# Selective scan: both rows copied to SBUF by ScalarE, and half of the B product on GpSimd in 18 of 64 units

## The reference, cut to what matters

```
states = states * exp(dt_t[:, :, None] * A) + dt_t[:, :, None] * B_t[:, None, :] * x_t[:, :, None]
y = einsum('bdn,bn->bd', states, C_t)
```

## Time and profile before

| | us |
|---|---|
| median of three runs | 2974.84 |
| lowest and highest run | 2967.43, 2976.77 |
| span of the profiled execution | 2973.1 |
| VectorE busy in the span | 2498.2 |
| state loop: first to last `times_b` starts | 2116.6 to 2364.2 |
| `times_b` L1864, 64 of them, busy | 76.8 |
| scans L1875, 128 of them, busy | 157.3 |
| `times_c` L1681, 63 of them, busy | 148.0 |

### The profile page before, as it was taken

One profiled execution on the slowest core, in us unless ns is written; L12 is line 12 of the kernel. 1 busy time (PEld: TensorE's weight loads), 2 busy tenths in 40 slices (PEclk: granted clock), 3 DMA queues, 4 the chain that ended last, 5 costly groups with the idle time before them and its releaser, 6 DMA issues.

```text
span 2973.1 us, 58047 instructions
## 1 busy us (share of the span) xinstructions
PE 2792.8 (94%) x23085; PEld 1251.6 (42%) x23085; DVE 2498.2 (84%) x3270; ACT 2081.2 (70%) x3906; POOL 881.3 (30%) x1050
## 2 busy tenths in 40 slices
PE   8999999999999989999999999999888799978889
PEld 2222222235666632222222356666333265467755
DVE  8999999976777689999999767776799956899854
ACT  6999999975666569999999766665777423735232
POOL 1000000012343310000000123433388655199810
PEclk9999999999999999999999999999999999989999
DMA  2000000000000010000000000000000000000000
GB/s 94 7 16 18 17 18 16 14 8 1 2 1 2 2 54 6 17 16 17 17 17 15 12 1 1 1 2 2 27 1 0 10 1 1 0 1 1 1 1 15
DMA packets 29148, 33.62 MB, mean 11 GB/s; under 512 B 13195, under 2 KB 23438, under 8 KB 28622
## 3 DMA queue, kind: packets, MB, share of 16 engines
q1 hardware_dynamic: 28878, 29.92, 3.5%
HBM read 17.58 MB, written 7.34 MB: 8 GB/s over the span
## 4 chain that ended last, share of the span: by engine, by line
PE 68%; DVE 19%; ACT 6%; issue 3%; POOL 2%; DMA 0%; SPq 0%; DVEq 0%; POOLq 0%; PEldq 0%; ACTq 0%
PE banks L401 15%; PE banks L383 10%; DVE max_parts L528 7%; PE banks L376 5%; PE banks L1114 3%; PE banks L2147 2%; PE banks L1025 2%; PE banks L2132 2%; PE banks L2134 2%; PE banks L1088 2%; PE banks L1133 2%; PE banks L1057 2%; ACT probs L644 2%; DVE banks L2998 2%; DVE state_keys L2995 2%
## 5 line engine op out<-in xcount | busy, mean ns | idle before, releaser
L528 DVE TENSOR_REDUCE max_parts<-banks 128x2 f32<-128x1024 f32 x1024 | 1170.7, 1217 | 11.5 <-PE banks L376 9.9
L644 ACT ACTIVATE probs<-banks 128x512 f32<-128x512 f32 x2048 | 1085.3, 599 | 59.8 <-PE banks L383 33.2
L383 PE MATMUL banks<-q_parts,k_parts 51*128 51x512 bf16 x2048 | 654.6, 385 | 4.8 <-ACT v_heads L603 1.5
L401 PE MATMUL banks<-probs,v_heads 128*9 128x256 f32 x8192 | 637.7, 383 | 8.2 <-ACT pv_copy L655 2.0
L376 PE MATMUL banks<-k_parts,q_parts 48*128 48x512 bf16 x2048 | 595.5, 385 | 10.5 <-DVE max_parts L528 6.0
L383 PEld LDWEIGHTS banks<-q_parts,k_parts 51*128 51x128 bf16 x2048 | 151.8, 94 | 474.7 <-ACT probs L644 397.1
L711 POOL CAST neg_max_parts<-neg_max 128x8 bf16<-128x8 f32 x64 | 13.0, 203 | 1122.5 <-DVE neg_max L533 1122.5
L401 PEld LDWEIGHTS banks<-probs,v_heads 128*9 128x9 f32 x8192 | 123.4, 88 | 382.0 <-issue 343.0
L1681 POOL TENSOR_TENSOR state_times_c<-state,c_row 128x1024 f32<-128x1024 f32 x63 | 148.0, 2354 | 88.8 <-ACT c_row L1997 54.2
L1875 DVE TENSOR_TENSOR_SCAN state<-banks,state_carry,state 128x512 f32<-128x512 f32 x128 | 157.3, 1271 | 6.4 <-ACT banks L1992 4.3
L2318 ACT ACTIVATE silu_a<-banks 128x512 f32<-128x512 f32 x80 | 47.7, 597 | 163.0 <-PE banks L2132 162.8
(11 more groups left out here) (526 smaller groups left out, 5053.3 us busy)
## 6 DMA issues: line engine op xcount, KB each, us to landing
outT_half<-pv_copy SPq DMA_DIRECT2D x248, 16.0 KB
prob_sums<-pv_copy SPq DMA_DIRECT2D x248, 2.0 KB
q_scratch<-qk_parts SPq DMA_DIRECT2D x8, 384.0 KB, 2.5
k_scratch<-qk_parts SPq DMA_DIRECT2D x8, 384.0 KB, 2.6
k_parts<-k_scratch SPq DMA_DIRECT2D x28, 96.0 KB
q_parts<-q_scratch SPq DMA_DIRECT2D x28, 96.0 KB
q_parts<-neg_max_rows SPq DMA_DIRECT2D x128, 3.0 KB
ffn_weights<-moe SPq DMA_DIRECT2D x1, 1928.0 KB, 7.6
```

Source lines behind the costliest of these rows:

```text
L383: nc.tensor.matmul(bank("exp", n, x)[:, :], K[p % 2][half_of(x, ROWS + PARTS), tile(t)], Q[p % 2][half_of(x, ROWS + PARTS), blk(j)], start ...
L401: i = nc.tensor.matmul(PVb[group:group + VD, cols], V[:, t + k, 2 * (s // NB) + x, :], PT[:, (n + k) % RING, x, cols], start=(t == 0 and c ...
L528: nc.vector.tensor_reduce(mxp[s % 2][:, :, u // NB, u % NB], Mb[m % 2].rearrange("p (x k) -> p x k", x=2), AX.X, ALU.max).then_inc(*maxed. ...
L644: nc.scalar.activation(PT[:, n % RING, x, :], bank("exp", n, x)[:, :], ACT.Exp, scale=float(HD) ** -0.5).then_inc(*exped.inc())
```

## The change

- The B row and the C row of a unit are spread by TensorE into two neighbouring banks (`spread`), two units ahead instead of one.
- ScalarE copies both rows with one 128x1024 copy to SBUF (`copy_bc`), in place of the 128x512 copy of the C row alone, also two units ahead, into one of four buffers `rows_of`.
- `times_b`, `times_c` and the last product read the rows from there. So `times_b` has both inputs in SBUF, and TensorE no longer waits for `times_b`, only for the copy.
- In 18 units GpSimd makes the upper half (c = 1) of the B product (`times_b_upper`), and VectorE's `times_b` only the lower. These are the units 2, 8 and 14 of the first block, 0, 2, 8 and 14 of the next two, and 0, 2, 6, 8, 10, 12 and 14 of the last. On GpSimd it is placed ahead of the `times_c` of the unit before. The second scan of a unit waits for it.

The diff, cut to its core:

```diff
+SHARED_WITH_FRONT, SHARED_IN_LAST = (0, 2, 8, 14), (0, 2, 6, 8, 10, 12, 14)
...
-        Cs, y = two("c_row", [128, 512]), two("scan_out", [128, 2, 512])
+        rows_of, y = [sb(f"bc_rows{i}", [128, 2, 512]) for i in range(4)], two("scan_out", [128, 2, 512])
...
-        Eb, Bb, Cb, Yb = g.ps[0:3], g.ps[3], g.ps[4], g.ps[5:7]
+        Eb, BCb, Yb = g.ps[0:3], g.wide(3), g.ps[5:7]
...
+        shared = [m for m in range(1, M) if m % NS in (SHARED_WITH_FRONT if m // NS + 1 < NB else SHARED_IN_LAST)]
+        n_shared = lambda m: len([k for k in shared if k <= m])
...
+            def times_b_upper(m):
+                pool.wait_ge(bc_copied, m + 1)
+                pool.wait_ge(dtx_made, m // NS + 1)
+                pool.wait_ge(c_times_state, m - 2)
+                pool.wait_ge(carried, m - 2)
+                nc.gpsimd.tensor_tensor(F[m % 3][:, 1, :], dtx[:, 1, unit_blk(m)], rows_of[m % 4][:, 0, :], ALU.mult).then_inc(*b_times_upper_x.inc())
...
             for m in range(M - 1):
                 b, n = m // NS, m % NS
+                if m + 1 in shared:
+                    times_b_upper(m + 1)
                 times_c(m)
...
-            def spread_b(m):
+            def spread(m):
                 pe.wait_ge(bc_low, m // NS + 1)
                 pe.wait_ge(mid_made, m // NS + 1)
-                pe.wait_ge(b_times_x, m)
-                nc.tensor.matmul(Bb[:, :], sel[:, m % NS, :], BC[:, unit_blk(m)], start=True, stop=True).then_inc(*b_spread.inc())
-
-            def spread_c(m):
-                pe.wait_ge(c_copied, m)
-                nc.tensor.matmul(Cb[:, :], sel[:, NS + m % NS, :], BC[:, unit_blk(m)], start=True, stop=True).then_inc(*c_spread.inc())
+                pe.wait_ge(bc_copied, m)
+                for k in range(2):
+                    i = nc.tensor.matmul(BCb[:, blk(k)], sel[:, NS * k + m % NS, :], BC[:, unit_blk(m)], start=True, stop=True)
+                i.then_inc(*bc_spread.inc())
...
             def times_b(m):
-                dve.wait_ge(b_spread, m + 1)
+                dve.wait_ge(bc_copied, m + 1)
                 dve.wait_ge(dtx_made, m // NS + 1)
                 dve.wait_ge(c_times_state, m - 2)
                 dve.wait_ge(carried, m - 2)
-                nc.vector.tensor_tensor(F[m % 3][:, :, :], dtx[:, :, unit_blk(m)], Bb[:, :].unsqueeze(1).broadcast_to([128, 2, 512]),
+                k = 1 if m in shared else 2
+                nc.vector.tensor_tensor(F[m % 3][:, 0:k, :], dtx[:, 0:k, unit_blk(m)], rows_of[m % 4][:, 0, :].unsqueeze(1).broadcast_to([128, k, 512]),
                                         ALU.mult).then_inc(*b_times_x.inc())
...
                     dve.wait_ge(decay_made, 2 * m + c + 1)
+                    if c == 1:
+                        dve.wait_ge(b_times_upper_x, n_shared(m))
...
-            def copy_c(m):
-                act.wait_ge(c_spread, m + 1)
-                act.wait_ge(c_times_state, m - 1)
-                nc.scalar.copy(Cs[m % 2][:, :], Cb[:, :]).then_inc(*c_copied.inc())
+            def copy_bc(m):
+                act.wait_ge(bc_spread, m + 1)
+                act.wait_ge(c_times_state, m - 3)
+                nc.scalar.copy(rows_of[m % 4][:, :, :].rearrange("p k t -> p (k t)"), BCb[:, :]).then_inc(*bc_copied.inc())
...
             decay(0)
-            copy_c(0)
+            copy_bc(0)
+            copy_bc(1)
```

More of the change, by code:

```diff
@@ L1624, in mamba @@
          dt_projected, dt_read, e_made, one_plus, log_made, u_back, rests_made, logs_made, dt_made, dtx_made) = s_front
-        s_loop = g.signals("b_spread c_spread decay_made c_copied b_times_x scanned carried c_times_state summed y_made y_gated last_product last_gated out_made x_added")
-        b_spread, c_spread, decay_made, c_copied, b_times_x, scanned, carried, c_times_state, summed, y_made, y_gated, last_product, last_gated, out_made, x_added = s_loop
+        s_loop = g.signals("bc_spread decay_made bc_copied b_times_x b_times_upper_x scanned carried c_times_state summed y_made y_gated last_product last_gated out_made x_added")
+        bc_spread, decay_made, bc_copied, b_times_x, b_times_upper_x, scanned, carried, c_times_state, summed, y_made, y_gated, last_product, last_gated, out_made, x_added = s_loop
         readers = dict(v0=(read_out, 4, 1), v1=(read_out, 4, 2), p2=(read_out, 4, 3), p3=(read_out, 4, 4),
@@ L1675, in times_x @@
                 nc.gpsimd.tensor_tensor(dtx[:, :, blk(b)], dt[:, :, blk(b)], xi[:, :, blk(b)], ALU.mult).then_inc(*dtx_made.inc())
+            def times_b_upper(m):
[4 more added lines that the diff above has]
+                nc.gpsimd.tensor_tensor(F[m % 3][:, 1, :], dtx[:, 1, unit_blk(m)], rows_of[m % 4][:, 0, :], ALU.mult).then_inc(*b_times_upper_x.inc())
             def times_c(m):
                 pool.wait_ge(scanned, 2 * m + 2)
-                pool.wait_ge(c_copied, m + 1)
+                pool.wait_ge(bc_copied, m + 1)
                 pool.wait_ge(summed, 2 * (m - 1))
-                nc.gpsimd.tensor_tensor(G[m % 2][:, :, :], F[m % 3][:, :, :], Cs[m % 2][:, :].unsqueeze(1).broadcast_to([128, 2, 512]),
+                nc.gpsimd.tensor_tensor(G[m % 2][:, :, :], F[m % 3][:, :, :], rows_of[m % 4][:, 1, :].unsqueeze(1).broadcast_to([128, 2, 512]),
                                         ALU.mult).then_inc(*c_times_state.inc())
@@ L1798, in on_pe @@
             pe.wait_ge(selected, 1)
-            spread_b(0)
-            spread_c(0)
+            spread(0)
+            spread(1)
             for m in range(M):
                 b, n = m // NS, m % NS
-                if m + 1 < M:
-                    spread_b(m + 1)
-                    spread_c(m + 1)
+                if m + 2 < M:
+                    spread(m + 2)
                 if b + 1 < NB:
@@ L1889, in last_product_of @@
                 dve.wait_ge(scanned, 2 * m + c + 1)
-                dve.wait_ge(c_copied, m + 1)
+                dve.wait_ge(bc_copied, m + 1)
                 dve.wait_ge(summed, 2 * (m - 1))
-                nc.vector.tensor_tensor(G[m % 2][:, c, :], F[m % 3][:, c, :], Cs[m % 2][:, :], ALU.mult).then_inc(*last_product.inc())
+                nc.vector.tensor_tensor(G[m % 2][:, c, :], F[m % 3][:, c, :], rows_of[m % 4][:, 1, :], ALU.mult).then_inc(*last_product.inc())
             def gate_last(c):
@@ L2033, in on_act @@
                     decay(m + 1)
-                    copy_c(m + 1)
+                    if m + 2 < M:
+                        copy_bc(m + 2)
                 if b + 1 < NB:
```

## The result

Four executions of the changed kernel took 3016.11 to 3025.56 us, median 3019.6, against 2974.32 for four of the kernel before on the same chip: a ratio of 1.0162, 95% interval 1.0145 to 1.0179, or 45.3 us more. The kernel is slower, as forecast, inside the range, and 14 us beyond the number predicted. The profiled execution took 3018.72 us, its span 3017.4, which is 44.3 over the span of the earlier trace rows. All of it lies in the state loop: the loop is 47.2 us longer, and what stands ahead of it was 3.3 shorter in this execution. First the page of the kernel after: the span, and busy time by engine.

The account below looks back on a forecast made before the run. VectorE, with next to no room in the state loop, was taken as the bound. Losses from blocking, less the waits that go, summed to +30.8 us on 2974.84: 3005.6 us, 8-in-10 range 2968 to 3024.

Parts of the forecast that it names:

- The question that decides: State loop: whether a VectorE product with two SBUF inputs and a GpSimd product exclude each other; claimed they do.
- A plain unit: State-loop unit without other GpSimd work behind `times_c`: costs nothing, `times_c` done at 3.38, before the next `times_b` at 3.60.
- The 15 long operations: `rests`, `correct_log`, `add_log`, `times_x` and `gate` on GpSimd behind `times_c`: 1.95 us lost each, 29.2 in all.
- The two splits: `split_rest` and `split_low` on GpSimd, 1.26 us each: cost 0.85 us each, six times, 5.1 in all.
- the waiting VectorE instruction goes first: Between two GpSimd instructions, a held VectorE product gets in, though the next GpSimd one started 0.04 us before.
- `add_x`: In two blocks of the state loop, hides about 0.6 us of the loss behind `split_rest` and `split_low`: -1.2 us.
- The halves: The 18 shared units: 15 lose 0.27 us each, 4.1 in all; three beside `finish` gain 0.53 each, -1.6.
- The decay of unit 3: VectorE's wait there grows about 0.5 us in two blocks, 0.2 in the last, shrinks 0.3 in the first: +0.9.
- What goes: VectorE's waits in the state loop that disappear: 6.0 us for the B row and 2.0 for the sums.
- The one without exclusion: Rival: no exclusion for this pair in the state loop, so 13.2 us faster, 2962 us; chance 0.12.
- the other rival: Rival: no exclusion, but the engines beside VectorE cap the state loop's gain at -7, 2968 us; chance 0.06.
- GpSimd gets there first: Rival: `times_c` wins at each scan's end, a unit takes 5.99 us, about 3125 us in all; chance 0.03.

Follow-up runs that it names:

- the rows alone: The changed kernel without the 18 shared halves, all 64 units reading both rows from SBUF: 3022.13 us, ratio 1.0159 to the kernel before.
- All three runs: Against the changed kernel: splits on 128 partitions, 3014.7 us; a completion wait behind each split, 3011.06 us; `rests` on 32 partitions in three blocks, 3041.02 us.
- the kernel with the added waits: The changed kernel with GpSimd waiting for the completion of each `split_rest` and `split_low` before going on: 3011.06 us, ratio 1.0125.
- The kernel with the short copies: The changed kernel with ScalarE copying the C row alone for units 2 and 3 of the three later blocks: 3022.54 us in one run.
- the kernel that writes zeros ahead of it: The changed kernel with `split_rest` and `split_low` on 128 partitions instead of 32, the added ones holding zeros: 3014.7 us, ratio 1.0134.

## Why the prediction was right, and where its sum was not

**The question that decides** was settled as predicted. With the rows in SBUF the pair excludes each other, with the B row in PSUM it does not, and the rows alone cost as much as the whole change. That the time lies inside the range is in part luck: the range's upper end stood for no overlap at all; the overlap was there, and the time came near that end by other terms.

**A plain unit** costs nothing: 3.61 us, `times_c` at 3.25 where 3.38 - 0.16 = 3.22 was worked out.

**The 15 long operations** at 1.95 us: `rests` and `correct_log` lengthen their unit by 1.98 to 2.00, six times. Of the 0.15 of overlap most held as well: `times_b` ends 1.08 behind `rests`, 0.12 less than its 1.20. Beside the Trainium skill (SBUF — State Buffer, section "Who interferes with whom"), whose rule taken literally came to 43 us, the measured 45 us are a near hit for another reason: the exclusion is as it says, the missing overlap is not, and what lifts the time to that number is the next term.

**The two splits are the step that failed.** The prediction had "the waiting VectorE instruction goes first", from the earlier trace rows, and so 0.85 us each. Units 7, 8 and 9 of the three blocks, where the splits and a shared half lie, grew by 4.02 - 0.53 + 3.24, 4.32 - 0.52 + 2.64 and 1.70 + 3.81 + 1.81, together 20.5 us. Of the third block's, 1.70 belongs to a `gate`, and 18.8 are left, where the prediction had 5.1 - 1.2 + 3 x 0.27 = 4.7. Behind the splits lie 17.0 of them, against 5.9 predicted with the three halves. The rule holds behind an operation on 128 partitions and fails behind one on 32: the kernels that change this, or that wait for the split's end, show it from both sides (5.22 to 1.70, and 3.19 to 7.79).

Why that is so is not seen in a trace, which shows GpSimd as one engine. The Trainium skill (GPSIMD Engine Reference, section "Instruction dispatch") says that GpSimd's cores serve 16 partitions each and that each begins the next instruction when its share of this one is done. By that, six of eight cores have nothing to do in a narrow operation and are in the next one before VectorE's turn can come; a wait for the completion brings them together again. All three runs agree with it, and so does the chain's end, in the two stretches shown, at an instruction that waits for a semaphore. Unit 8 of the third block agrees too: VectorE's half asks 1.43 us into the `times_c` behind the split, an operation on 128 partitions, and still waits for two more (5.01 us); in the kernel with the added waits it asks 1.33 into the same `times_c`, goes behind it and takes 1.57. There VectorE gets its turn ahead of `split_low`, for which the trace shows no wait, so what ends a chain is not settled.

**`add_x`**, put at -1.2, is the other 1.8. In the second block it did hide 0.6 (unit 9 takes 3.85 there and 4.43 in the first block, which has no `add_x`). In the third it gave GpSimd the lead, as the lines above show, and `times_b` took 3.02. This does not come from the splits: in the kernel of the rows alone `times_b` takes 3.02 behind `add_x` in the last block too, where there are no splits.

**The halves**: 0.39 us lost in a unit where a half stands alone (units 10, 12 and 14 of the last block), 0.27 predicted; the three beside `finish` gain 0.53 as predicted. Unhindered a half takes 1.26 to 1.28, not 1.21.

**The decay of unit 3** was put at +0.9 for all blocks; the four units grew by 1.26, 0.96, 0.96 and 0.83, 4.0 us. The halved `times_b` was counted and the longer copy was not: the prediction hid it behind ScalarE's idle time of a tight stretch, but ahead of the table loads there is none. The kernel with the short copies shows this share, 0.35 to 0.43 us in a block. The largest miss is the first block, 1.26 where -0.3 was predicted; 0.7 of it went away in a kernel that changed nothing there, with TensorE's clock.

**What goes**, 8.0 us predicted: the B row's waits all went, and 1.7 us of those for the sums. The second number is luck in part: with the rows alone the sums were waited for 4.5 us, 3.1 of them ahead of one `finish`, with TensorE's clock at 0.50. The 1.0 at the loop's start is the 1.1 in the waits; the joint copy took 1.00 where 1.05 was taken. The 1.3 for reading the row from SBUF did not come: where nothing holds it, `times_b` takes 1.20, as from PSUM.

The loop grew by 47.2 us where the sum, without the 1.0 ahead of its first `times_b`, has 29.8. Of the 17.4 between them the units of the splits are 14.1 (11.1 behind the splits, 3.0 at `add_x`) and the decay 3.1; the other terms miss both ways, and their misses cancel. In the profiled executions the loop also began at 2113.3 instead of 2116.6, which makes up the span's 44.3; over the kernels of this study it began anywhere between 2110.7 and 2122.1. The latest is the kernel that writes zeros ahead of it; for the others no run says why.

**The rivals.** The one without exclusion is refuted: its condition was a `times_c` of 2.36 beside a `times_b` from SBUF. Its gain of 9.5 us was real in the kernels that keep the B row in PSUM, and there the other rival's point came true: the engines beside VectorE take it all back. "GpSimd gets there first" did not happen in plain units, at a margin of 0.17 us, but happens behind narrow operations and behind `add_x`. That TensorE's clock costs the time, which fell from 0.96 to 0.88 over the loop, is not borne out: in the lists of its waits VectorE waits 1.5 us for TensorE in the loop after, and 9.2 before.

## What to carry to other kernels

Before an operand is moved from PSUM to SBUF to free a bank or to let another engine read it, look at what runs beside its reader: here 64 products lost their independence of GpSimd to give 18 of them a helper. A VectorE product with two SBUF inputs waits for one GpSimd operation, and for the whole run of them if the first used 32 of the 128 partitions; here a wait for that one's completion, or all 128 partitions, gave the turn back. And an engine relieved of 9.5 us gains nothing when the engines that feed it are only just on time.

## What the runs showed of the hardware that was not expected

A GpSimd operation on 32 partitions takes as long as the same on 128 (2.35 us for 32x1024 and for 128x1024; 1.14 for 32x512 and 1.15 for 128x512) and does more harm: VectorE's product took 2.0 us longer behind one on 128, and 6.6 behind the same on 32, through two more instructions. Two GpSimd instructions of 128 partitions in a row do let VectorE in between, though the second starts 0.04 us before the first one's end, unless one on 32 stands ahead of them with no wait since. And a completion wait behind a short operation, which would seem to cost GpSimd time, took 8.5 us off the kernel after (intervals 1.011 to 1.0139 and 1.0145 to 1.0179).
